# A vision tower's attention product in half-precision splits, tokens per column half, and steps moved in the tail

## The chip, the cores and the metric

The kernel runs on one core of a Trainium2 chip. The metric is the device time of one execution in microseconds, from the launch on the core to its end; the smaller the better. A core has TensorE (matrix products, accumulating in eight PSUM banks, here `bank[0]` to `bank[7]`), VectorE, ScalarE, GpSimd and the DMA queues of SyncE and GpSimd. Each engine works through its own list of instructions in order; they meet at semaphores, where one engine waits until another has counted up.

## The reference

Eight images of 3 x 256 x 256 in float32 go through three steps, with 256 tokens of 256 numbers per image:

```
gray  = weighted sum of the three colours
h     = (|scharr_x * gray| + |scharr_y * gray|) / 2      # 3x3 convolutions: tokens
Q,K,V = h Wq' + bq, h Wk' + bk, h Wv' + bv
h     = layernorm(h + softmax(causal(Q K' / 16)) V)
p     = softmax(h Wr);  e = argmax(p);  pos = rank of the token among those of e
kept  = pos < 320                                          # capacity of an expert
out   = where(kept, relu(h W1[e]) W2[e], h) * where(kept, max(p), 1)
h     = layernorm(h + out)
```

There are eight experts (256 to 1024 and back) with 320 slots each.

## The kernel before

**Halves.** A float32 matrix product takes TensorE several passes. Nearly all products are therefore made of two halves: `hi` is the number written in the type float32r, `lo` is the rest, number minus `hi`, and a product is hi hi + hi lo + lo hi, three matmuls of a faster kind. ScalarE writes a `hi` (ACTIVATE with Copy), and VectorE then the `lo` (a subtraction). The attention product, softmax weights times values, is the exception: `attend` (L1347) makes it of three full-precision matmuls, one for the first 128 tokens and two for the others, each with 264 columns (256 values and 8 gate columns, `XG`).

**The order of the work.** There are no planners: the source is five hand-written lists, one per engine, and the order of calls in a list is the order in time. In the attention stage, the loop `for i in range(B)` takes image i through attention, while image i+1 is convolved and i-1 is normalised and routed. On TensorE (L1380 on) it runs `project_keys(i)` (three terms of four matmuls; the third wants `xT_lo`), `project_values(i)`, `scores(i)` (three terms, the third wants the low keys, `yT_ready`), `count(i-1)`, the convolution of image i+1 for the two column halves of the picture (`convolve`, six groups of six matmuls; between the fifth and the sixth stand the transposes of the softmax weights, `prob_t`), `attend(i)` and `tokens_as_rows(i+1)`, four transposes of the tokens.

The steps of the other engines that the prediction names, with the names of the list and the tile as the profile shows it:

| step | engine, line | what it does |
|---|---|---|
| edges | ScalarE L609 | absolute value of one column half of the convolution, PSUM to `edges_abs` (in `tokens_mem`) |
| tokens | VectorE L907 | sum of both edge directions to `xT`, for both column halves at once |
| tokens_high, tokens_low | ScalarE L616, VectorE L912 | halves of `xT` (tiles `w_hi`, `w_lo`, which lend their space) |
| gray_high, gray_low | ScalarE L598, VectorE L860 | halves of the gray picture i+1 |
| project_keys, keys_low | ScalarE L623, VectorE L934 | halves of the keys with their bias, from bank 3 |
| project_values, row_constant | ScalarE L633, L639 | values out of PSUM to `val`; a constant per row |
| softmax_max | VectorE L959, L966 | scaled, masked scores and their maximum |
| probs, prob_t | ScalarE L649, L672 | exponentials; transposed weights out of bank 7 |
| route, residual, moments, assign, factor | VectorE L1009, L985, L992, L1036, L1029 | choice of expert, residual, layernorm statistics, slot of a token, gate factor |
| residual_in | VectorE L928 | token rows plus the value bias |
| route_exp, norm_rows, norm_lone | ScalarE L701, L680, L689 | exponentials of the gate; rows to scatter; rows for tokens without a slot |
| red_and_green, scale_blue, add_blue | VectorE L855, ScalarE L591, GpSimd L520 | gray picture i+2 |
| tally, scatter, scale_rows, scale_lone | GpSimd L498, L512, L465, L477 | running counts; two indirect DMAs that write an image's rows to their slots in DRAM; layernorm scales |
| split_high, split_low | ScalarE L712, VectorE L919 | halves of a quarter of an expert's weights, 128x1024 |

VectorE's list for image i is route(i-1), gray_low(i+1), factor(i-2), keys_low(i), residual(i-1), softmax_max(i), moments(i-1), residual_in(i), assign(i-1), softmax_sum(i), red_and_green(i+2), tokens(i+1), tokens_low(i+1). ScalarE's is gray_high(i+1), project_keys, project_values, row_constant, scale_blue(i+2), norm_lone(i-2), probs(i), edges(i+1, 0), prob_t(i), edges(i+1, 1), route_exp(i-1), tokens_high(i+1), norm_rows(i-1). The weights of expert 0 are split for the first time in images 5 and 6.

**The tail.** The last image, 7 (`L`), has a list of its own: `late_prob_t`, `late_attend`. Expert 0 gets its tokens partly from DRAM (`early_turn`, L1436, in which blocks of token rows are multiplied by the identity in full precision) and, for images 6 and 7, directly by `place` (L1423), a full-precision product of the rows with a 0/1 matrix `pick` that VectorE makes by comparisons in `assign`. Then the expert stage begins (L1208 to L1210), eight experts one after another.

## Time and profile before

| | us |
|---|---|
| median of three runs | 260.03 |
| lowest, highest | 259.54, 262.11 |
| the profiled execution | 262.5 |
| its span | 260.7 |
| busy: TensorE, VectorE, ScalarE, GpSimd | 243.5, 182.4, 155.3, 98.4 |

The profile is of one execution. A row of a timeline begins with the start in us from the beginning of the span and the duration; rows that follow one another closely are merged, with their number behind x. In brackets stands how long the engine was idle before it and which instruction ended the wait. Neighbouring instructions of an engine overlap by their fill and drain: the start of the next row, not the end of this one, gives the pace. The attention stage reaches from about 20 to 121 us, the expert stage to the end.

### The profile page before, as it was taken

The numbers are of one execution on the slowest core, as the hardware profiler recorded it, in microseconds if no ns is written. First come the engines' busy times: TensorE is split into PE (matmuls) and PEld (weight loads), VectorE is DVE, ScalarE is ACT, GpSimd is POOL, SyncE is SP. The second block draws the span as 40 slices with busy tenths as digits, with TensorE's granted clock in tenths as the row PEclk, the third lists the DMA queues.
The fourth block names the chain that finished last, engine by engine and source line by source line (L and its number), as shares of the span: only waits on it lengthen the run. The fifth ranks groups of instructions, "written<-read, shape, count | busy, mean of one in ns | idle before, by whom it ended". The sixth has DMA issues, their size and how long they took to land.

```text
span 260.7 us, 5010 instructions
## 1 busy us (share of the span) xinstructions
PE 243.5 (93%) x1690; PEld 227.9 (87%) x1690; DVE 182.4 (70%) x544; ACT 155.3 (60%) x351; POOL 98.4 (38%) x172
## 2 busy tenths in 40 slices
PE   6999999999999899898999999999999999999930
PEld 5999898989898798776999999999999999999930
DVE  4845496968778987965756696777967678777530
ACT  4325556776768687475645568474774748655400
POOL 6000116655665655646100025034250332513473
PEclk9989999999999999999999999999999999999995
DMA  6947192346595201041799807337092450100000
GB/s 191 268 120 252 28 299 52 115 137 226 179 373 186 73 20 60 29 131 41 199 261 334 298 5 263 112 97 259 0 296 78 150 203 3 46 0 23 10 27 0
DMA packets 28122, 35.48 MB, mean 136 GB/s; under 512 B 2652, under 2 KB 24907, under 8 KB 28098
## 3 DMA queue, kind: packets, MB, share of 16 engines
q1 hardware_dynamic: 26016, 31.71, 37.8%
q0 software_dynamic: 1792, 3.47, 3.7%
q8 instruction: 13, 0.21, 0.3%
q14 instruction: 11, 0.09, 0.1%
q10 hardware_dynamic: 290, 0.00, 0.1%
HBM read 26.97 MB, written 9.47 MB: 140 GB/s over the span
## 4 chain that ended last, share of the span: by engine, by line
PE 84%; DVE 6%; issue 3%; ACT 2%; POOL 2%; POOLq 1%; DMA 0%; ACTq 0%; DVEq 0%
PE bank L1208 16%; PE bank L1210 15%; PE bank L1209 15%; PE bank L1280 14%; PE bank L1296 5%; PE bank L1333 4%; PE bank L1455 3%; DVE xT L907 2%; PE bank L1506 2%; PE bank L1430 2%; PE bank L1370 2%; PE bank L1307 2%; ACT tokens_mem L609 1%; POOL out_dram L552 1%; PE bank L1216 1%
## 5 line engine op out<-in xcount | busy, mean ns | idle before, releaser
L1137 DVE SCALAR_TENSOR_TENSOR h_lo<-bank,h_hi 128x320 fp32r<-128x320 f32 x58 | 28.4, 490 | 29.3 <-ACT h_hi L782 25.5
L782 ACT ACTIVATE h_hi<-bank 128x320 fp32r<-128x320 f32 x58 | 25.4, 438 | 38.3 <-PE bank L1210 38.0
L1208 PE MATMUL bank<-einT_hi,w_hi 128*128 128x320 f32 x128 | 40.5, 317 | 0.3 <-DVE h_lo L1137 0.2
L1210 PE MATMUL bank<-einT_hi,w_lo 128*128 128x320 f32 x128 | 39.6, 309 | 0.0
L1209 PE MATMUL bank<-einT_lo,w_hi 128*128 128x320 f32 x128 | 39.5, 309 | 0.0
L919 DVE TENSOR_TENSOR w_lo<-w_raw,w_hi 128x1024 fp32r<-128x1024 f32 x32 | 38.9, 1216 | 0.0
L552 POOL DMA_INDIRECT out_dram<-tokens_mem,images x24 | 27.4, 1143 | 28.4 <-ACT tokens_mem L799 22.2
L1208 PE MATMUL bank<-h_hi,w_hi 128*128 128x320 f32 x112 | 35.4, 316 | 0.1
L1209 PE MATMUL bank<-h_lo,w_hi 128*128 128x320 f32 x112 | 34.6, 309 | 0.0
L1210 PE MATMUL bank<-h_hi,w_lo 128*128 128x320 f32 x112 | 34.6, 309 | 0.0
L712 ACT ACTIVATE w_hi<-w_raw 128x1024 fp32r<-128x1024 f32 x32 | 33.7, 1054 | 1.2 <-DMA w_raw<-in_L_ffn_W_dram 1.2
L546 POOL TENSOR_TENSOR yrstd<-yve,minus_half 128x3 f32<-128x3 f32 x7 | 6.2, 880 | 60.9 <-DVE yve L1167 60.7
L1208 PEld LDWEIGHTS bank<-einT_hi,w_hi 128*128 128x128 f32 x128 | 24.1, 188 | 1.0 <-DVE h_lo L1137 0.4
L1209 PEld LDWEIGHTS bank<-einT_lo,w_hi 128*128 128x128 f32 x128 | 24.1, 188 | 0.0
L1210 PEld LDWEIGHTS bank<-einT_hi,w_lo 128*128 128x128 f32 x128 | 24.0, 188 | 0.0
L1208 PEld LDWEIGHTS bank<-h_hi,w_hi 128*128 128x128 f32 x112 | 21.0, 188 | 0.8 <-issue 0.3
L1209 PEld LDWEIGHTS bank<-h_lo,w_hi 128*128 128x128 f32 x112 | 21.1, 188 | 0.0
L1210 PEld LDWEIGHTS bank<-h_hi,w_lo 128*128 128x128 f32 x112 | 21.0, 188 | 0.0
L512 POOL DMA_INDIRECT dispatched<-trow,slot x16 | 16.4, 1026 | 8.5 <-issue 7.8
L609 ACT ACTIVATE tokens_mem<-bank 128x512 f32<-128x512 f32 x16 | 9.6, 599 | 10.5 <-PE bank L1280 10.5
L1280 PE MATMUL bank<-w_hi 128*128 128x260 f32 x96 | 15.6, 300 | 0.0
L907 DVE TENSOR_TENSOR xT<-tokens_mem 128x512 f32<-128x512 f32 x8 | 6.7, 843 | 12.0 <-ACT tokens_mem L609 12.0
(228 smaller groups left out, 598.9 us busy)
## 6 DMA issues: line engine op xcount, KB each, us to landing
w_raw<-in_L_ffn_W_dram SPq DMA_DIRECT2D x16, 1024.0 KB
images<-in_x_dram SPq DMA_DIRECT2D x7, 768.0 KB, 5.0
dispatched<-blank SPq DMA_DIRECT2D x4, 645.0 KB, 8.7
images<-dispatched SPq DMA_DIRECT2D x9, 258.0 KB, 3.3
out_dram<-lone SPq DMA_DIRECT2D x8, 256.0 KB, 3.6
images<-in_x_dram SPq DMA_DIRECT2D x2, 384.0 KB, 4.9
images<-dispatched SPq DMA_DIRECT2D x9, 64.5 KB, 3.7
out_dram<-tokens_mem,images POOLq DMA_INDIRECT x24
```

Source lines behind the costliest of these rows:

```text
L512: pool.indirect_dma_start(dispatched, bass.IndirectOffsetOnAxis(ap=slot[:, b % TR, s:s + 1], axis=0), trow[:, b % TR, s, :], None, bounds_ ...
L552: pool.indirect_dma_start(out_rows, bass.IndirectOffsetOnAxis(ap=ein[0:n, e, j, D + 1:D + 2].bitcast(U32), axis=0), z[0:n, e % 2, j, :], N ...
L609: act.activation(edges_abs[:, c].rearrange("p f s -> p (f s)"), bank[c][:, :], ACT.Abs).then_inc(edges_ready, 1)
L712: act.activation(w_hi[:, e % 2, c], w_raw[:, e % 2, c], ACT.Copy).then_inc(w_hi_ready, 1)
L782: act.activation(hidden_halves(n)[0], bank[n % 2][:, 0:CAP], ACT.Relu).then_inc(h_hi_ready, 1)
L919: dve.tensor_tensor(w_lo[:, e % 2, c], w_raw[:, e % 2, c], w_hi[:, e % 2, c].bitcast(F32), ALU.subtract).then_inc(w_lo_ready, 1)
L1137: dve.scalar_tensor_tensor(lo, bank[n % 2][:, 0:CAP], 0.0, hi.bitcast(F32), ALU.max, ALU.subtract).then_inc(h_ready, 1)
L1208: pe.matmul(to, ah, bh, start=first, stop=False)
L1209: pe.matmul(to, ah, bl, start=False, stop=False)
L1210: return pe.matmul(to, al, bh, start=False, stop=last)
L1280: ins = pe.matmul(acc[:, :, s * (S - REACH):s * (S - REACH) + REACH], half[:, b % 2, s, c * P + dx:c * P + dx + P], of_band[:, dx, :, 2 - ...
L1296: ins = pe.matmul(bank[3][:, c * S:(c + 1) * S], half[:, k, c * P:(c + 1) * P], of_x[:, b % 2, k, :], start=(t == c == k == 0), stop=(t == ...
```

## The change

The attention product of images 0 to 5 is made by `attend_halves`: nine matmuls of the halves of the transposed weights and of the values. ScalarE writes the high halves (`values_high`, `prob_t_high`, the latter in place of `prob_t`), VectorE the low ones (`values_low`, `prob_t_low`). Images 6 and 7 keep the full-precision product. `edges`, `tokens`, `tokens_high`, the key projection's first term and `tokens_as_rows` now go by column half, with a semaphore count for each.

Steps are moved: on ScalarE gray_high behind project_keys, norm_lone behind probs, and the weight splits of image 5 to image 6; on VectorE the first token half ahead of assign, red_and_green behind the second token half, factor from the next image's list to behind red_and_green, and in the tail softmax_max ahead of moments, route ahead of factor, and `base` behind the comparisons; on GpSimd scatter ahead of tally; on TensorE early_turn ahead of place, now as real transposes, and two idle-filling matmuls (`keep_warm(2)`) are gone.

```diff
@@ -159,6 +161,8 @@
         probT = sb("probT", [P, S + P])
+        probT_hi = sb("probT_hi", [P, S + P], F32R)
+        probT_lo = sb("probT_lo", [P, S + P], F32R)
@@ -520,10 +528,10 @@
             for i in range(B):
+                if i >= 2:
+                    scatter(i - 2)
                 if i >= 1:
                     tally(i - 1)
-                if i >= 2:
-                    scatter(i - 2)
                 gate_tokens(i)
@@ -604,16 +612,28 @@
                 if b >= 1:
-                    act.wait_ge(xT_ready, b)
+                    act.wait_ge(xT_ready, DC * (b - 1) + c + 1)
                 act.wait_ge(conv_done, DC * b + c + 1)
...
-            def tokens_high(b):
-                act.wait_ge(xT_ready, b + 1)
+            def tokens_high(b, c):
+                act.wait_ge(xT_ready, DC * b + c + 1)
                 if b >= 2:
                     act.wait_ge(scores_done, b - 1)
-                act.activation(xT_hi[:, b % 2], xT[:, b % 2], ACT.Copy).then_inc(xT_hi_ready, 1)
+                act.activation(xT_hi[:, b % 2, c], xT[:, b % 2, c], ACT.Copy).then_inc(xT_hi_ready, 1)
+
+            def values_high(b):
+                if b >= 1:
+                    act.wait_ge(attn_done, b)
+                act.wait_ge(rowc_ready, b + 1)
+                act.activation(val_hi[:, :, :], val[:, b % 2, :, 0:XG], ACT.Copy).then_inc(val_hi_ready, 1)
+
+            def prob_t_high(b):
+                act.wait_ge(pT_done, b + 1)
+                if b >= 1:
+                    act.wait_ge(attn_done, b)
+                act.activation(probT_hi[:, :], bank[7][:, 0:S + P], ACT.Copy).then_inc(probT_hi_ready, 1)
@@ -730,31 +750,37 @@
             gray_high(1)
-            tokens_high(0)
+            for c in range(DC):
+                tokens_high(0, c)
             act.wait_ge(setup_ev, 1)
             for i in range(B):
+                project_keys(i)
                 if 1 <= i < L:
                     gray_high(i + 1)
-                project_keys(i)
                 project_values(i)
...
                 elif i < L:
-                    split_high(1)
+                    split_high(0)
                 if i == L:
                     break
+                if i < L - 1:
+                    values_high(i)
+                probs(i)
                 if i >= 2:
                     norm_lone(i - 2)
-                probs(i)
                 edges(i + 1, 0)
-                if i == L - 2:
-                    split_high(0)
-                prob_t(i)
+                tokens_high(i + 1, 0)
+                if i == L - 1:
+                    split_high(1)
+                    prob_t(i)
+                else:
+                    prob_t_high(i)
                 edges(i + 1, 1)
+                tokens_high(i + 1, 1)
                 if i >= 1:
                     route_exp(i - 1)
-                tokens_high(i + 1)
                 if i >= 1:
@@ -899,16 +925,26 @@
-            def tokens(b):
-
-                dve.wait_ge(edges_ready, DC * (b + 1))
+            def tokens(b, c):
+
+                dve.wait_ge(edges_ready, DC * b + c + 1)
                 if b >= 2:
                     dve.wait_ge(scores_done, b - 1)
-                dve.tensor_tensor(xT[:, b % 2], edges_abs[:, :, 0, :], edges_abs[:, :, 1, :], ALU.add
+                dve.tensor_tensor(xT[:, b % 2, c], edges_abs[:, c, 0, :], edges_abs[:, c, 1, :], ALU.add
                                   ).then_inc(xT_ready, 1)
+            def values_low(b):
+                dve.wait_ge(val_hi_ready, b + 1)
+                dve.tensor_tensor(val_lo[:, :, :], val[:, b % 2, :, 0:XG], val_hi[:, :, :].bitcast(F32), ALU.subtract
+                                  ).then_inc(val_lo_ready, 1)
+
+            def prob_t_low(b):
+                dve.wait_ge(probT_hi_ready, b + 1)
+                dve.tensor_tensor(probT_lo[:, :], bank[7][:, 0:S + P], probT_hi[:, :].bitcast(F32), ALU.subtract
+                                  ).then_inc(probT_lo_ready, 1)
+
             def tokens_low(b):
-                dve.wait_ge(xT_hi_ready, b + 1)
+                dve.wait_ge(xT_hi_ready, DC * (b + 1))
                 dve.tensor_tensor(xT_lo[:, b % 2], xT[:, b % 2], xT_hi[:, b % 2].bitcast(F32), ALU.subtract
@@ -1034,13 +1070,16 @@
                 step(dve.tensor_tensor(mine[:, :, :], onehot[:, b % 2], count, ALU.mult))
-                step(dve.tensor_scalar(base[:, :], best[:, b % 2], -float(CAP), float(E * CAP - 1),
-                                       ALU.mult, ALU.add))
+                if b < L - 1:
+                    step(dve.tensor_scalar(base[:, :], best[:, b % 2], -float(CAP), float(E * CAP - 1),
+                                           ALU.mult, ALU.add))
                 settle()
...
                                           ).then_inc(pick_ready, 1)
+                    step(dve.tensor_scalar(base[:, :], best[:, b % 2], -float(CAP), float(E * CAP - 1),
+                                           ALU.mult, ALU.add))
                 link(dve.tensor_reduce(place[:, :], mine[:, :, :], AX_X, ALU.add))
@@ -1069,7 +1108,8 @@
             make_gray(1)
-            tokens(0)
+            for c in range(DC):
+                tokens(0, c)
             gray_low(1)
@@ -1087,8 +1127,6 @@
                     gray_low(i + 1)
-                if i >= 2:
-                    factor(i - 2)
                 keys_low(i)
@@ -1097,29 +1135,36 @@
                 residual_in(i, 1)
+                tokens(i + 1, 0)
                 if i >= 1:
                 softmax_sum(i)
+                if i < L - 1:
+                    values_low(i)
+                    prob_t_low(i)
+                else:
+                    split_low(0)
+                tokens(i + 1, 1)
                 if i + 2 < B:
                     red_and_green(i + 2)
-                if i >= L - 2:
-                    split_low(i - L + 2)
-                tokens(i + 1)
+                if i >= 1:
+                    factor(i - 1)
+                if i == L - 1:
+                    split_low(1)
                 tokens_low(i + 1)
             route(L - 1)
-            factor(L - 2)
             residual(L - 1)
             keys_low(L)
+            softmax_max(L)
             moments(L - 1)
-            softmax_max(L)
             assign(L - 1)
             moments(L)
+            route(L)
             factor(L - 1)
-            route(L)
             assign(L)
@@ -1285,25 +1330,26 @@
             def project_keys(b):
-                pe.wait_ge(xT_hi_ready, b + 1)
                 if b >= 1:
...
                         pe.wait_ge(xT_lo_ready, b + 1)
-                    for c in range(DC):
-                        for k in range(DC):
+                    for k in range(DC):
+                        if t == 0:
+                            pe.wait_ge(xT_hi_ready, DC * b + k + 1)
+                        for c in range(DC):
                             ins = pe.matmul(bank[3][:, c * S:(c + 1) * S], half[:, k, c * P:(c + 1) * P],
...
             def tokens_as_rows(b):
-                pe.wait_ge(xT_ready, b + 1)
                 if b >= 1:
                     pe.wait_ge(xb_ready, b)
-                for s in range(SC):
-                    for c in range(DC):
+                for c in range(DC):
+                    pe.wait_ge(xT_ready, DC * b + c + 1)
+                    for s in range(SC):
                         ins = pe.transpose(bank[2][:, s * D + c * P:s * D + (c + 1) * P],
@@ -1344,8 +1390,23 @@
+            def attend_halves(b):
+                pe.wait_ge(probT_hi_ready, b + 1)
+                pe.wait_ge(val_hi_ready, b + 1)
+                for t, (p, v) in enumerate(((probT_hi, val_hi), (probT_hi, val_lo), (probT_lo, val_hi))):
+                    if t == 1:
+                        pe.wait_ge(val_lo_ready, b + 1)
+                    if t == 2:
+                        pe.wait_ge(probT_lo_ready, b + 1)
+                    for k in range(SC):
+                        pe.matmul(bank[5][:, 0:XG], p[:, (k + 1) * P:(k + 2) * P], v[:, k, :],
+                                  start=(t == k == 0), stop=(t == 2 and k == SC - 1))
+                for t, (p, v) in enumerate(((probT_hi, val_hi), (probT_hi, val_lo), (probT_lo, val_hi))):
+                    ins = pe.matmul(bank[7][:, 0:XG], p[:, 0:P], v[:, 0, :], start=(t == 0), stop=(t == 2))
+                ins.then_inc(attn_done, 1)
+
             def attend(b):
-                pe.wait_ge(probT_ready, b + 1)
+                pe.wait_ge(probT_ready, 1)
                 pe.matmul(bank[7][:, 0:XG], probT[:, 0:P], val[:, b % 2, 0, 0:XG], start=True, stop=True)
@@ -1394,7 +1455,10 @@
                     convolve(i + 1, 1, (2,))
-                    attend(i)
+                    if i < L - 1:
+                        attend_halves(i)
+                    else:
+                        attend(i)
                     tokens_as_rows(i + 1)
@@ -1408,7 +1472,7 @@
             def late_attend():
-                pe.wait_ge(probT_ready, L + 1)
+                pe.wait_ge(probT_ready, 2)
                 pe.matmul(bank[5][:, 0:XG], probT[:, P:2 * P], val[:, L % 2, 0, 0:XG], start=True, stop=False)
@@ -1421,31 +1485,29 @@
             def place(b):
-                if b == L - 1:
-                    pe.wait_ge(rowc_ready, B)
                 for c in range(DC):
...
                         ins = pe.matmul(bank[c][:, 0:CAP], trow[:, b % TR, s, c * P:(c + 1) * P], pick(b, s),
-                                        start=(b == L - 1 and s == 0), stop=(b == L and s == SC - 1),
+                                        start=False, stop=(b == L and s == SC - 1),
                                         skip_group_check=True)
...
             def early_turn():
+                pe.wait_ge(rowc_ready, B)
                 pe.wait_ge(ein_in[0], 32)
                         ins = pe.matmul(bank[c][:, o:o + n], ein[0:n, 0, j, c * P:(c + 1) * P], ident[0:n, 0:n],
-                                        start=False, stop=False, skip_group_check=True)
+                                        start=(j == 0), stop=False, is_transpose=True, skip_group_check=True)
                 ins.then_inc(early_turned, 1)
+            early_turn()
             place(L - 1)
-            early_turn()
             count(L)
             place(L)
-            keep_warm(2)
                 pe.wait_ge(ein_in[e], 32)
```

## Rows read from the trace of the kernel before

**Rows 1.** the trace's windows: each engine's busy us, then PEclk, DMA share, GB/s.

```profile
52.00:104.00 52.00, 50.70 (x387) 46.26 (x386) 41.29 (x160) 38.18 (x106) 31.50 (x57) 1.00 0.46 157
```

**Rows 2.** timeline of TensorE, image 4: start us, us, instruction, count, idle before.

```profile
68.61 0.64 PE L1296 MATMUL bank<-w_lo,w_hi 128*128 128x256 f32 x4
...
71.54 0.62 PE L1333 MATMUL bank<-w_hi,w_lo 128*128 128x128 f32 x4
...
76.94 0.71 PE L1349 MATMUL bank<-val,probT 128*128 128x264 f32 x2
...
78.65 0.66 PE L1307 MATMUL bank<-ident,xT 128*128 128x128 f32 x4
```

**Rows 3.** chain of waits in order of time: start us, us, what.

```profile
76.36 0.73 PE bank L1280 x6
```

**Rows 4.** timeline of VectorE, image 4.

```profile
69.48 0.69 DVE L860 TENSOR_TENSOR w_lo<-red,w_hi 128x512 fp32r<-128x512 f32 x1
...
70.17 0.88 DVE L934 SCALAR_TENSOR_TENSOR w_lo<-bank,key_bias,w_hi 128x256 fp32r<-128x256 f32 x2
...
72.19 0.29 DVE L959 CUSTOM_DVE_ANT_0 tokens_mem<-bank,causal 128x128 f32<-128x128 f32 x1 [0.37 <-PE bank L1333]
...
75.06 0.16 DVE L1036 TENSOR_TENSOR mine<-onehot,bank 128x16 f32<-128x16 bf16 x1
...
75.96 0.67 DVE L855 SCALAR_TENSOR_TENSOR red<-images 128x512 f32<-128x512 f32 x1
...
77.80 0.80 DVE L907 TENSOR_TENSOR xT<-tokens_mem 128x512 f32<-128x512 f32 x1 [1.16 <-ACT tokens_mem L609]
```

**Rows 5.** timeline of ScalarE, image 4.

```profile
68.39 0.61 ACT L598 ACTIVATE w_hi<-red 128x512 fp32r<-128x512 f32 x1
...
69.29 0.84 ACT L623 ACTIVATE w_hi<-bank,key_bias 128x256 fp32r<-128x256 f32 x2 [0.28 <-PE bank L1296]
...
72.20 0.93 ACT L689 ACTIVATE lone<-trow,lone_scale 128x256 f32<-128x256 f32 x2
...
74.67 0.60 ACT L609 ACTIVATE tokens_mem<-bank 128x512 f32<-128x512 f32 x1 [0.56 <-PE bank L1280]
...
77.17 0.60 ACT L609 ACTIVATE tokens_mem<-bank 128x512 f32<-128x512 f32 x1 [0.28 <-PE bank L1280]
...
78.14 0.19 ACT L701 ACTIVATION_READ_ACCUMULATOR lexp<-lsub,rstd 128x1 f32 x1
```

**Rows 6.** timeline, image 5, and instances of line L520: ns min/median/max, first and last start.

```profile
86.94 1.05 ACT L712 ACTIVATE w_hi<-w_raw 128x1024 fp32r<-128x1024 f32 x1
...
88.32 1.22 DVE L919 TENSOR_TENSOR w_lo<-w_raw,w_hi 128x1024 fp32r<-128x1024 f32 x1
...
L520 POOL TENSOR_TENSOR red<-red,images x6: 1266/1270/2112, 28.2 to 88.6; 128x512 f32<-128x512 f32 x6
...
89.60 1.61 DVE L907 TENSOR_TENSOR xT<-tokens_mem 128x512 f32<-128x512 f32 x1
...
91.27 0.66 PE L1307 MATMUL bank<-ident,xT 128*128 128x128 f32 x4 [0.93 <-DVE xT L907]
```

**Rows 7.** part 5 of the page: busy us, mean ns, idle us before it.

```profile
L512 POOL DMA_INDIRECT dispatched<-trow,slot x16 | 16.4, 1026 | 8.5 <-issue 7.8
```

**Rows 8.** timeline of TensorE, the first images.

```profile
20.24 0.63 PE L1307 MATMUL bank<-ident,xT 128*128 128x128 f32 x4 [0.27 <-DVE xT L907]
...
31.66 0.65 PE L1307 MATMUL bank<-ident,xT 128*128 128x128 f32 x4
```

**Rows 9.** timeline of the tail of the attention stage.

```profile
111.50 0.71 PE L1412 MATMUL bank<-val,probT 128*128 128x264 f32 x2 [0.19 <-ACT probT L664]
...
112.94 2.32 PE L1430 MATMUL bank<-tokens_mem,trow 128*128 128x320 f32 x8
...
115.09 1.97 PE L1440 MATMUL bank<-ident,images 128*128 128x128 f32 x12
...
117.32 0.17 DVE L1036 TENSOR_TENSOR mine<-onehot,bank 128x16 f32<-128x16 bf16 x1 [0.92 <-PE bank L1365]
```

More of the change, by code:

```diff
@@ L151, in vit_tower_kernel @@
         val = sb("val", [P, 2, SC, VCOLS - 2])
+        val_hi = sb("val_hi", [P, SC, XG], F32R)
+        val_lo = sb("val_lo", [P, SC, XG], F32R)
         gate_in = sb("gate_in", [P, 2, SC, E])
@@ L227, in vit_tower_kernel @@
         mean_done = sem("mean_done")
+        val_hi_ready = sem("val_hi_ready")
+        val_lo_ready = sem("val_lo_ready")
+        probT_hi_ready = sem("probT_hi_ready")
+        probT_lo_ready = sem("probT_lo_ready")
         late_probs_ready = sem("late_probs_ready")
```

## The prediction

> **What bounds the kernel now.** I read first the busy time and the granted clock of the stretch in which images 1 to 6 go through attention, then that stretch's timeline engine by engine, then the places where VectorE and GpSimd overlap, then the tail. TensorE is busy 50.70 of 52 us at full clock [rows 1]: the period of an image is the length of TensorE's work, and anything that makes TensorE wait is paid in full. The expert stage after it is one unbroken run of matmuls, so it passes a shift on and absorbs none. The attention stage decides.
>
> I use two marks for one image i (numbers of image 4 and the start of 5). Y is the end of its key projection: the third product starts at 68.61 and ends 0.64 later, 69.25 [rows 2]. S is the start of its softmax maximum on VectorE, 72.19, right behind the last score product [rows 2, 4]. From Y to S are 2.94 us. From S on, the next image's convolution ends when the attention product starts, 76.94 or S+4.75; the token transposes start at 78.65 and last 0.66, so they end at S+7.12 [rows 2]. Eight key matmuls later, at S+8.18, the low half of the tokens is needed, and Y of the next image is S+8.82.
>
> **The attention product.** Full-precision matmuls of 264 columns: three took 112.94 - 111.50 = 1.44 us in the late copy of this product [rows 9]. The half-precision convolution matmul has 260 columns and takes 0.73 / 6 = 0.122 us in the chain of waits [rows 3]; an upper end is 0.64 / 4 = 0.16, the last drain counted in, for the 256 columns of the key product [rows 2]. Nine are 1.10 to 1.44 us; I take 1.11, by the chain's row, whose columns are nearest. TensorE alone saves 0.33 us, and, as the transposes today also wait for xT (77.80 + 0.80 = 78.60, where 76.94 + 1.44 is 78.38) [rows 4], up to 0.25 more, since xT now comes in halves. Six images at 0.58: 3.5 us is the most that this part can give.
>
> **What the halves cost VectorE.** New work between S and the last token half: a 128x528 subtraction, between 0.67 us (512 elements, two tensor inputs, row of 75.96) and 1.22 (1024) [rows 4, 6], by size 0.71; a 128x384 subtraction from PSUM, between the 0.44 of one and the 0.88 of two subtractions of 256 from there (row of 70.17) [rows 4], by size 0.54; and the second start of the split xT, two pieces of about 0.4 (half of 0.67, and a start) against one of 0.80. The line of VectorE: from S to the end of the residual input it is 75.06 - 72.19 = 2.87. There it now waits for the first token half. ScalarE does the lone rows after the exponentials instead of before (0.93, the row of 72.20) [rows 5]. The exponentials end at 74.67 - 0.56 = S+1.92, so lone rows end at S+2.86 and the edges at S+3.46 instead of 75.27 = S+3.08. So tokens from S+3.48, then assign and sum (75.96 - 75.06 = 0.90), and the low values start at S+4.72 and are done at S+5.43; low probabilities, started 0.62 later, are done at S+5.90; the second token half at S+6.22. TensorE wants the low values at S+5.0 and the low probabilities 0.25 after those: it waits 0.45 and 0.2, ends attention at S+6.56 and the transposes at S+7.2. Against S+7.12: **+0.08 us an image**. The whole saving is eaten by the waits. Splitting the tokens' high copy costs ScalarE about 0.15 and lies in its idle time, for between the edges of 74.67 and of 77.17 it has only the probabilities' copy [rows 5], so I cost it at nothing; without that cover it would delay the high probabilities by as much.
>
> **The low tokens.** Red-and-green (0.67) is now between the second token half and the low tokens, and so is the factor, which waits for the routing exponentials. Those follow the second high copy on ScalarE: from S+6.57 to S+7.24 (0.66, from 77.77 less the overlap of 0.1 to 78.14 + 0.19) [rows 5]. The low tokens could start at S+7.38 and end at S+8.1, in time for S+8.26. But the blue plane's addition on GpSimd starts when red-and-green ends, about S+6.95, and its median is 1.27. Where it did meet two-tensor subtractions of VectorE, it took 2.11 from 88.6, while the subtraction of 88.32 kept its 1.22; then the xT of 89.60 took 1.61 in place of 0.80, and TensorE waited 0.93 [rows 6]. That is one waiting for the other, first GpSimd, then VectorE: behind the subtraction's end at 89.54 the addition still took 1.15. So here the low tokens really start at about S+8.1 and are done at S+8.75: **+0.6 us** an image for images 2 to 4, 0.5 in the first. Today the addition lies in VectorE's idle 1.16 us.
>
> The Trainium skill, "SBUF — State Buffer", section "SBUF: two separate sides", calls the ports that VectorE shares with GpSimd an exclusive lock, held for the whole instruction by whichever starts first, a VectorE operation with two SBUF inputs or a GpSimd one that reads SBUF. By that rule the low tokens wait as above; by free sharing they would not, and the sum would be the third case below. By that rule, the trace agrees.
>
> **The gray halves, in the other order.** ScalarE's gray_high moves behind project_keys; VectorE's gray_low stays before keys_low. Today gray_high runs at 68.39, before Y [rows 5], gray_low at 69.48, and keys_low at 70.17 [rows 4], as soon as the high keys (69.29 + 0.84) are there; it ends at 71.05, 0.49 before the third score product wants it at 71.54 [rows 2]. Now: high keys Y+0.79 in pitch, gray_high to Y+1.40, gray_low 0.6, keys_low from Y+2.02, done Y+2.90, where Y+2.29 is wanted. TensorE waits 0.61, scores end at Y+3.56, and the residual (0.79) puts S at Y+3.60 against 2.94. **+0.66 us for each of images 1 to 6: 3.96.** Nothing covers it: behind the scores, TensorE has only the count and the convolution queued.
>
> **Moved steps.** The two scattering transfers of an image, (16.4 + 8.5) / 8 = 3.1 us of GpSimd with their gaps [rows 7], now stand before the tally. With the addition later they run from about S+10 to S+13, the tally ends at S'+0.9 of the next image; its users (counts, one image later) and the next row scaling (S'+2.4) come after it: nothing. SP only waits on those landings at the end. Image 5 no longer carries a weight split, so what its wait of 0.93 is above the others' goes [rows 6]: **-0.85**, less the 0.6 above. Image 6 carries both: on ScalarE the second split (1.05) [rows 6] stands before the probabilities' copy, which ends about S+5.7 instead of S+4.7, so the full-precision attention starts 1 us late; on VectorE a split of 1.22 stands before the low tokens, done at S+9.55, wanted at S+8.9. Y comes at S+10.2 against about S+8.75: **+1.5**. Image 0 has neither lone rows nor factor: transposes end at about 31.84 against 31.66 + 0.66 [rows 8]: **-0.48**. Before it, the 0.27 us wait for xT [rows 8] goes: **-0.25**.
>
> **The tail.** Today early_turn takes 1.91 us behind place (115.09 to 117.0) and the count of image 7 stands behind it, while VectorE, done with the one-hot at 117.32 - 0.92 = 116.40, waits for the count [rows 9]. As six transposes (0.66 / 4 each) in front of place it takes 1.0: 0.5 off. Base behind the comparisons gives 0.2. Maximum before moments would give 0.4 on the critical side, but keys_low comes 0.3 later, and moments then stands before the last residual: +0.3. **-0.6** in sum. The two warming matmuls had filled a wait: nothing.
>
> **Sum.** -0.25 - 0.48 + 3.96 + 0.5 + 3 x 0.6 + (0.6 - 0.85) + 1.5 - 0.6 = +6.2 us. It is made on the profiled execution (262.5 us, span 260.7, so 1.8 around it), which is 2.5 us above the median of the runs, 260.03; the difference is put on the median: **266.2 us**.
>
> **Rivals.** (a) *Everything covered, faster.* If gray_low and the low halves landed before TensorE wants them, 0.58 would be won per image: the sum with -0.58 in place of the terms of images 1 to 5, no 3.96, gives -3.6, 256.4. It decides at keys_low done by Y+2.29: it would need 0.6 us less between Y and keys_low, and both orders and durations speak against it. For it: VectorE has 1.16 us idle per image in one piece [rows 4]. 0.08. (b) *Only gray binds*: the low values and probabilities arrive by S+5.25, say because the edges are not delayed and subtractions run nearer their lower bounds, and the low tokens slip in before the addition. Then -2.3 - 1.4 for images 1 to 5 against 3.96 and 1.5 and the ends: +0.4, 260.4. 0.12. (c) *No lock between VectorE and GpSimd*: the low tokens are on time, images 1 to 4 cost about nothing and image 5 gives 0.75: +3.5, 263.5. Against it stands the overlap [rows 6], for it only that it is one event. 0.15. (d) *TensorE's clock falls in the new waits*, about 1.3 us an image in three or four pieces. The clock has two levels, 1.2 and 2.4 GHz; the stretch shows only the upper. Against it: 0.93 of idle at 90.3 left the clock at 1.00 [rows 1, 6]. One convolution part of 0.73 at half speed per image is 4.4 on top: 270.6. 0.08. The forecast keeps 0.57, by itself 264.5 to 268.5: the ends are the 528-element subtraction up to 0.98 (+0.27 x 5) and matmuls of 0.16 (+0.3 x 5) above, and a lock that costs only half below.
>
> **Numbers.** About 1% (2.6 us) is what a measurement can tell from none. Faster by it: 0.08, case (a). Within: 0.14, case (b) and a corner of (c). Slower: 0.78, the rest. The range, 260 to 269, leaves out (a), (d) and some of (b).
>
> **What the profile after would show.** TensorE waiting before the third score product for keys_low (w_lo), about 0.6 us, six times; before the second and third attention products; before the third key product for the low tokens, those lasting about 1.3 in place of 0.7 beside the blue addition; image 7's key projection ending some 7 us later than 105.3; the count no longer behind early_turn. The prediction is wrong if the third score product starts without a wait, or if the period from image to image stays at or under 11.8 us.

## The result and the profile after

The changed kernel takes 268.18 us (median of four runs, 267.75 to 268.64); the kernel before, on the same chip, 259.95. The ratio is 1.027, with a 95% interval of 1.022 to 1.033: 8.2 us slower, where 6.2 were forecast. The profiled execution took 267.75 us with a span of 266.0. Executions of every kernel here fall on two levels, 2.3 us apart (262.0 and 259.7 us for the kernel before), of which the profiles show the upper one with 0.50 and the lower one with 1.00 of TensorE's clock granted from 13 to 15 us, ahead of the attention stage; the profile before lies on the upper level and all four executions of the changed kernel on the lower, so "at equal starts" below means medians of the lower level. The spans of the two profiles therefore differ by 5.3 us only, and I compare them by marks inside the attention stage.

The window of the attention stage, in the columns of [rows 1]:

```profile
52.00:104.00 52.00, 46.87 (x369) 43.60 (x369) 43.84 (x162) 36.19 (x103) 27.47 (x55) 1.00 0.47 157
```

TensorE is busy 46.87 of 52 us in place of 50.70, at the same clock; VectorE 43.84 in place of 41.29. The work shrank and the waits grew. The timeline of TensorE shows them for the same image as [rows 2]:

```profile
68.86 0.74 PE L1342 MATMUL bank<-w_lo,w_hi 128*128 128x256 f32 x4 [0.77 <-DVE w_lo L948]
...
72.56 0.73 PE L1379 MATMUL bank<-w_hi,w_lo 128*128 128x128 f32 x4 [0.52 <-DVE w_lo L970]
...
78.08 0.51 PE L1402 MATMUL bank<-val_hi,probT_hi 128*128 128x264 f32 x2
...
78.54 0.51 PE L1402 MATMUL bank<-val_lo,probT_hi 128*128 128x264 f32 x2
...
79.01 0.51 PE L1402 MATMUL bank<-val_hi,probT_lo 128*128 128x264 f32 x2
...
79.72 0.60 PE L1353 MATMUL bank<-ident,xT 128*128 128x128 f32 x4
...
80.07 0.72 PE L1342 MATMUL bank<-w_hi 128*128 128x256 f32 x4
```

The third key product waits 0.77 us for the low tokens, the third score product 0.52 us for the low keys (w_lo of line 970). In [rows 2] the key and score products had no wait. From one set of transposes to the next (66.53 to 79.72) it is 13.19 us; before, the marks Y of images 4 and 5 lay 11.76 us apart.

Within the attention product the second and third groups start 0.46 and 0.47 us after the one before. What they need without a wait is seen in image 0, where both lows come in time:

```profile
26.75 0.51 PE L1402 MATMUL bank<-val_hi,probT_hi 128*128 128x264 f32 x2
27.10 0.41 PE L1402 MATMUL bank<-val_lo,probT_hi 128*128 128x264 f32 x2
27.35 0.51 PE L1402 MATMUL bank<-val_hi,probT_lo 128*128 128x264 f32 x2
...
28.06 0.60 PE L1353 MATMUL bank<-ident,xT 128*128 128x128 f32 x4
```

There the steps are 0.35 and 0.25, and the whole product takes 1.31 us (26.75 to 28.06). In image 4 it takes 1.64 (78.08 to 79.72): 0.11 of waiting for the low values and 0.22 for the low weights. VectorE and then GpSimd in image 4, as in [rows 4] and [rows 6]:

```profile
67.28 0.17 DVE L1065 RECIPROCAL trow<-lsum 128x2 f32<-128x2 f32 x1 [0.45 <-ACT lexp L721]
...
67.36 1.44 DVE L948 TENSOR_TENSOR w_lo<-xT,w_hi 128x512 fp32r<-128x512 f32 x1
...
71.02 0.69 DVE L886 TENSOR_TENSOR w_lo<-red,w_hi 128x512 fp32r<-128x512 f32 x1 [0.89 <-ACT w_hi L606]
...
71.63 0.87 DVE L970 SCALAR_TENSOR_TENSOR w_lo<-bank,key_bias,w_hi 128x256 fp32r<-128x256 f32 x2
...
77.80 0.69 DVE L938 TENSOR_TENSOR val_lo<-val,val_hi 128x528 fp32r<-128x528 f32 x1
...
78.40 0.55 DVE L943 TENSOR_TENSOR probT_lo<-bank,probT_hi 128x384 fp32r<-128x384 f32 x1
```

```profile
66.97 1.28 POOL L528 TENSOR_TENSOR red<-red,images 128x512 f32<-128x512 f32 x1 [3.12 <-DVE red L881]
```

The low tokens (line 948) take 1.44 us in place of 0.7 because the blue addition has been running since 66.97. gray_low (line 886) comes behind 0.89 us of idleness, keys_low only behind it. The low values (0.69) and low weights (0.55) stand one behind the other at 77.80; the first are done at 78.49, and TensorE wanted them at 78.43.

The last loss is in no part of the attention stage. A timeline of all engines where it ends:

```profile
122.21 1.21 POOL L520 DMA_INDIRECT dispatched<-trow,slot  x1 [1.45 <-ACT trow L700]
...
127.33 1.24 DVE L955 TENSOR_TENSOR w_lo<-w_raw,w_hi 128x1024 fp32r<-128x1024 f32 x1
...
127.56 1.06 POOL L486 TENSOR_TENSOR v2n<-v,mv 128x2 f32<-128x2 f32 x1
...
128.98 1.70 POOL L490 TENSOR_TENSOR lone_scale<-v2e,minus_half 128x2 f32<-128x2 f32 x1
...
130.71 0.91 ACT L709 ACTIVATE lone<-trow,lone_scale 128x256 f32<-128x256 f32 x2 [2.56 <-POOL lone_scale L490]
...
132.52 0.42 PE L1253 MATMUL bank<-einT_hi,w_hi 128*128 128x320 f32 x1 [0.93 <-DVE h_lo L1182]
```

GpSimd's scatter of image 6 starts at 122.21. Its small scale operations therefore come at 127.56 and 128.98, beside weight splits on VectorE (one is the row of 127.33), and take 1.06 and 1.70 us. In the kernel before, the same two took 0.20 and 1.75 there, so only the first meeting is new; the first scale operation also comes 0.8 us later, counted from the first expert product. ScalarE writes the last lone rows behind them, the hidden block of expert 0 stands behind those, and TensorE waits 0.93 us.

### The profile page after: what moved, and what is told of

Its sections match the earlier page's. It is cut to its first block, busy times and chain, and to the rows that moved or that the text cites. A ratio compares the mean times of both kernels' runs of the same rounds, so it can differ in the third digit from the quotient of the medians.

```text
span 266.0 us, 5088 instructions
## 1 busy us (share of the span) xinstructions
PE 240.7 (90%) x1700; PEld 225.7 (85%) x1700; DVE 193.3 (73%) x564; ACT 159.3 (60%) x365; POOL 95.9 (36%) x172
## 4 chain that ended last, share of the span: by engine, by line
PE 44%; DVE 6%; POOL 5%; issue 4%; ACT 2%; POOLq 1%; DVEq 0%; ACTq 0%
PE bank L1253 14%; PE bank L1255 13%; PE bank L1254 13%; PE bank L1517 3%; PE bank L1568 2%; POOL out_dram L560 1%; POOL dispatched L520 1%; DVE resid L1021 1%; POOL yrstd L583 1%; POOL lone_scale L490 1%; POOLq L67 1%; PE bank L1379 1%; DVE stats L1028 1%; DVE w_lo L955 0%; DVE w_lo L970 0%
## 5 line engine op out<-in xcount | busy, mean ns | idle before, releaser
L520 POOL DMA_INDIRECT dispatched<-trow,slot x16 | 16.5, 1034 | 9.3 <-ACT trow L700 5.6
L528 POOL TENSOR_TENSOR red<-red,images 128x512 f32<-128x512 f32 x6 | 8.1, 1345 | 23.3 <-DVE red L881 23.3
L1325 PE MATMUL bank<-w_hi 128*128 128x260 f32 x96 | 14.9, 291 | 0.0
L1325 PE MATMUL bank<-w_lo,w_hi 128*128 128x260 f32 x96 | 14.9, 291 | 0.0
```

Source lines behind the costliest of these rows:

```text
L520: pool.indirect_dma_start(dispatched, bass.IndirectOffsetOnAxis(ap=slot[:, b % TR, s:s + 1], axis=0), trow[:, b % TR, s, :], None, bounds_ ...
L528: pool.tensor_tensor(red[:, b % 2], red[:, b % 2], pix[:, b % 2, 2], ALU.add).then_inc(gray_ready, 1)
L1325: ins = pe.matmul(acc[:, :, s * (S - REACH):s * (S - REACH) + REACH], half[:, b % 2, s, c * P + dx:c * P + dx + P], of_band[:, dx, :, 2 - ...
```

## The experiments

Diffs are against the changed kernel unless said otherwise. Ratios are to the kernel before, run in between on the same chip. The changed kernel itself was not run again beside them; at equal starts the kernel before reads 259.9, 259.8, 259.7 and 259.7 us in the four sessions, so a difference of two or three tenths from its 268.2 means nothing.

**e1_gray_first: one order undone.**

```diff
-                project_keys(i)
                 if 1 <= i < L:
                     gray_high(i + 1)
+                project_keys(i)
```

> The changed kernel (268.2 us) with gray_high again ahead of project_keys on ScalarE, nothing else. Theory (each of the six low-key waits of TensorE, 0.52 us, and the 0.2 us by which the residual then delays the softmax, is caused by this order): the wait before the third score product goes, the period falls from 13.18 to about 12.4 us, the time to about 263.5 us (-4.7). Rival 1 (VectorE is simply too loaded; the wait moves to the next place): the period stays above 12.9 and the time above 266.5. Rival 2 (the low tokens behind the blue addition set the period alone): no change.

264.5 us, ratio 1.014 (1.006 to 1.022): 3.7 us less. No third score product of images 1 to 6 waits any more, and the marks of the third key product lie 12.4 us apart. The low tokens keep their wait:

```profile
67.93 0.74 PE L1342 MATMUL bank<-w_lo,w_hi 128*128 128x256 f32 x4 [0.79 <-DVE w_lo L948]
```

The theory holds: images 2 to 6 gain 0.79 us each, as expected. Image 1 gains only 0.25, since it has a new wait of 0.31 for the high keys, and 4.2 us are won between the first and the last token transposes. The rest of the gap to the 4.7 expected is no effect of the edit: those first transposes start at 17.77 in this profile and at 16.87 in that of the changed kernel, though the steps ahead of them are the same.

**e2_low_first: low tokens ahead of what had been put in front of them.**

```diff
                 tokens(i + 1, 1)
+                tokens_low(i + 1)
                 if i + 2 < B:
                     red_and_green(i + 2)
                 if i >= 1:
                     factor(i - 1)
                 if i == L - 1:
                     split_low(1)
-                tokens_low(i + 1)
```

> The changed kernel with tokens_low directly behind the second token half on VectorE, ahead of red_and_green, factor and the second weight split. Theory (the low tokens are late because they stand behind red_and_green and then wait for the blue addition on GpSimd): the waits before the third key product (0.87, 0.72, 0.77, 0.77, 0.77 and, for image 7, 0.90 us) go, low tokens take 0.7 us instead of 1.45, time about 263.6 us (-4.6). Rival (the wait for high keys and gray halves behind it absorbs an earlier start): under 1.5 us gained.

263.85 us, ratio 1.010 (1.006 to 1.014): 4.3 less. All six waits before the third key product are gone, those before the third score product stay and are longer, 0.61 to 0.98 us in images 1 to 6:

```profile
70.67 0.73 PE L1379 MATMUL bank<-w_hi,w_lo 128*128 128x128 f32 x4 [0.65 <-DVE w_lo L970]
```

**e4_factor_first: the tail's factor put back.**

```diff
-            route(L)
             factor(L - 1)
+            route(L)
             assign(L)
```

> The changed kernel with factor(L-1) again ahead of route(L) in the tail of VectorE. Theory: GpSimd's scatter of image 6 waits for this factor; it started at 122.2 instead of about 119.9, so the scale of the last lone rows met two weight splits on VectorE (1.06 and 1.70 us) and ScalarE, with norm_lone in front of the second hidden block, held TensorE for 0.93 us. Then the scatter starts some 1.2 us earlier or more, that wait goes, and the time falls by about 1.2 us to 267.0. Rival (the wait comes from image 7's rows, which end GpSimd's queue anyhow, or from weight splits): no change.

267.0 us, ratio 1.022 (1.015 to 1.029): 1.2 less, and the wait of 0.93 is gone. The timeline shows how:

```profile
121.69 1.08 POOL L520 DMA_INDIRECT dispatched<-trow,slot  x1 [0.70 <-ACT trow L700]
...
127.09 0.19 POOL L486 TENSOR_TENSOR v2n<-v,mv 128x2 f32<-128x2 f32 x1
...
127.65 1.69 POOL L490 TENSOR_TENSOR lone_scale<-v2e,minus_half 128x2 f32<-128x2 f32 x1
...
129.37 0.91 ACT L709 ACTIVATE lone<-trow,lone_scale 128x256 f32<-128x256 f32 x2 [1.00 <-POOL lone_scale L490]
```

The scatter starts only 0.5 us earlier than at 122.21, less than I had expected. That is enough for the first small operation to slip in ahead of the split (0.19 us, not 1.06); the lone rows come 1.34 us earlier. One meeting is avoided, the other (1.69) stays, as in the kernel before.

**e5_blue_waits: the contention by itself.** One more wait, no operation moved within its engine.

```diff
                 pool.wait_ge(warm_ready, b - 1)
+                pool.wait_ge(xT_lo_ready, b)
```

> The changed kernel with one more wait: GpSimd's blue addition starts only when the low tokens of the image are done. No operation is removed or reordered within an engine. Theory (the low tokens, 1.45 us, wait inside their own time for the addition, which holds ports that both need): they take about 0.7 us, TensorE's wait before the third key product falls from 0.77 to about 0.1, the time by 0.65 us for each of images 2 to 6, to about 265 us. Rival (the low tokens are slow for another reason, or wait for the factor only): duration and time unchanged, or later because the gray picture comes later.

265.0 us, ratio 1.016 (1.009 to 1.024): 3.1 us less by adding a wait. The low tokens and the addition in this kernel:

```profile
66.22 0.67 DVE L949 TENSOR_TENSOR w_lo<-xT,w_hi 128x512 fp32r<-128x512 f32 x1
...
67.06 1.29 POOL L529 TENSOR_TENSOR red<-red,images 128x512 f32<-128x512 f32 x1 [4.35 <-DVE w_lo L949]
```

0.67 us in place of 1.44, and TensorE waits before no third key product but that of image 7. The theory holds. The transposes lie 12.4 us apart in place of 13.18, 0.78 an image where 0.65 was expected; the first ones start 0.4 us later than in the profile of the changed kernel.

**g4_before_gray: the gray order alone, on the kernel before.**

```diff
+                project_keys(i)
                 if 1 <= i < L:
                     gray_high(i + 1)
-                project_keys(i)
```

> The kernel before with one move alone: gray_high(i+1) behind project_keys(i) on ScalarE. Theory (the order by itself makes the low keys 0.6 us late and the residual behind them delays the softmax): 0.66 to 0.75 us for each of images 1 to 6, together +4.0 to +4.5 us, ratio about 1.016; TensorE waits 0.5 us before the third score product six times. Rival (in the kernel before the wait for xT would shrink by as much, or the chip needs the heavier VectorE line of the changed kernel to show it): under 1.5 us.

266.1 us, ratio 1.018 (1.011 to 1.025). Six waits of 0.52 to 0.58 before the third score product, as forecast. At equal starts (264.8, two executions, against 259.7) it is 5.1 us, a little more than forecast.

**g2_halves_only: the half-precision product alone, on the kernel before**, with norm_lone behind the first edges.

```diff
                 softmax_sum(i)
+                if i < L - 1:
+                    values_low(i)
+                    prob_t_low(i)
                 if i + 2 < B:
                     red_and_green(i + 2)
...
-                    attend(i)
+                    if i < L - 1:
+                        attend_halves(i)
+                    else:
+                        attend(i)
```

> The kernel before with the half-precision attention product of images 0 to 5 alone (and norm_lone behind the first edges, to make room for values_high); tokens whole, no step moved but that. VectorE makes the low values and weights behind softmax_sum, ahead of red_and_green and tokens. Theory (TensorE saves 0.33 us an image, but then waits for xT, which is now as late as before or later because 1.1 us of subtractions stand ahead of it): within 1 us of the kernel before. Rival (the saving arrives in full): 0.33 x 6 = 2 us faster.

264.2 us, ratio 1.014 (1.009 to 1.019): 4.4 us slower at equal starts, which neither theory had. Rows of TensorE, of VectorE, again of TensorE, and the window behind it (the columns of [rows 1]):

```profile
76.53 0.66 PE L1345 MATMUL bank<-ident,xT 128*128 128x128 f32 x4 [0.33 <-DVE xT L932]
...
89.34 1.75 DVE L932 TENSOR_TENSOR xT<-tokens_mem 128x512 f32<-128x512 f32 x1
...
91.15 1.12 PE L1345 MATMUL bank<-ident,xT 128*128 128x128 f32 x4 [2.52 <-DVE xT L932]
```

```profile
91.00:94.00 3.00, 2.85 (x14) 2.86 (x15) 2.17 (x11) 2.13 (x4) 1.93 (x5) 0.50 0.00 0
```

The product is shorter, but the transposes wait 0.33 us for xT in each of images 0 to 4, as the theory says: 0.17 an image slower than e6_tail_only, whose attention stage is that of the kernel before, 0.85 in all. What it missed is image 5, which carries a weight split on VectorE: the blue addition takes 2.11 us between that split and xT, xT takes 1.75, and TensorE waits 2.52 us in place of 0.93. From transposes to transposes image 5 takes 2.0 us more. Behind that wait TensorE is granted 0.50, the lower of its two levels, from 91 to 94 us: from the start of the transposes to the first value product it is 3.36 us (91.15 to 94.51), where the kernel before needs 2.20 at 1.00. The clock takes another 1.2 us. The three add up to 4.0, the difference of the two spans. How much of image 5's loss is the split rather than the halves was not separated; the kernel before had that split and the wait of 0.93 too, and kept its clock.

**e7_full: the changed kernel with the full-precision product.**

```diff
-                    if i < L - 1:
-                        attend_halves(i)
-                    else:
-                        attend(i)
+                    attend(i)
```

(and no values_high, values_low, prob_t_high, prob_t_low)

> The changed kernel with the full-precision attention product for all images again (no attend_halves, no high and low halves of values and weights), every moved step and the column halves of the tokens kept. Theory: TensorE pays 0.33 us more per image, but VectorE is 1.2 us lighter and ScalarE 0.6, so the low tokens come earlier by about 0.2 to 0.5; about 267.3 us, 0.5 to 1.5 less than the changed kernel: the halves gave nothing here. Rival (the halves are a gain that the moved steps hide): 2 us more, 270.

269.3 us, ratio 1.031 (1.027 to 1.035), 269.1 at equal starts against 268.2: 0.9 more, where I had expected less. The sign is a miss. In images 2 to 6 the period is the same 13.18 us, with 0.95 in place of 0.77 of waiting for the low tokens. From the first transposes to image 2's third key product it is 0.4 us longer, and the wait of 0.93 in the expert stage is 1.20.

**f1_best and f2_best_lone: three orders mended, then a fourth.**

```diff
-                if 1 <= i < L:
-                    gray_low(i + 1)
                 keys_low(i)
                 if i >= 1:
                     residual(i - 1)
+                if 1 <= i < L:
+                    gray_low(i + 1)
...
-                if i >= 2:
-                    norm_lone(i - 2)
                 edges(i + 1, 0)
+                if i >= 2:
+                    norm_lone(i - 2)
```

(with the moves of e2 and e4; the second hunk only in f2_best_lone. The gray order is mended on the other side here: gray_high stays, and VectorE's gray_low goes behind the low keys.)

> The changed kernel with three orders mended together: gray_low on VectorE behind keys_low and residual (gray_high stays behind project_keys), tokens_low directly behind the second token half, factor(L-1) ahead of route(L). Theory (the three effects are separate and add: -3.7, -4.3, -1.2 as measured one by one): about 259 us, at or 1 us under the kernel before. Rival (the same slack is counted twice): above 262.

> The kernel f1_best with norm_lone on ScalarE behind the first edges instead of ahead of them, so that the first token half comes 0.4 us earlier on VectorE and the low values and low weights with it. Theory (TensorE waits inside the attention product because VectorE's line from the softmax maximum is too long, and the edges were 0.4 of it): 0.4 us less per image of 2 to 5, about 257.4 us. Rival (the inner waits cost nothing since the token halves set the end): same as f1_best.

f1_best: 260.3 us, ratio 0.995 (0.992 to 0.997). f2_best_lone: 258.6, ratio 0.992 (0.988 to 0.995). At equal starts it is 260.2 and 258.5 against 259.7. The three effects, 3.7, 4.3 and 1.2, would give 259.0 if they added; they fall 1.3 us short. The period is 11.9 us in f1_best, still above the 11.76 before: the attention product waits for the low values 0.33 us in each of images 2 to 5. With the edges moved it is 11.54, which is the 0.4 an image that was expected: 1.7 us.

**f3_full_same_order: what the halves are worth, once the orders are right.** f2_best_lone with the full-precision product.

> The kernel f2_best_lone (258.6 us) with the full-precision attention product for all images, every order kept. Theory: with the three orders mended the period is TensorE's work again, so the product's own 0.33 us an image is what the halves give: 1.5 to 2 us more than f2_best_lone, 260.3. Rival (VectorE's 1.2 us of subtractions still hold TensorE as much as they save): the same as f2_best_lone or faster.

258.9 us, ratio 0.993 (0.990 to 0.997), not to be told from f2_best_lone; the rival had it. The attention product and the transposes behind it in f2_best_lone, then here, with the third score product of the same image:

```profile
73.56 0.50 PE L1402 MATMUL bank<-val_hi,probT_hi 128*128 128x264 f32 x2
...
74.14 0.51 PE L1402 MATMUL bank<-val_lo,probT_hi 128*128 128x264 f32 x2
...
75.32 0.60 PE L1353 MATMUL bank<-ident,xT 128*128 128x128 f32 x4
```

```profile
68.37 0.73 PE L1372 MATMUL bank<-w_hi,w_lo 128*128 128x128 f32 x4
...
73.90 0.71 PE L1403 MATMUL bank<-val,probT 128*128 128x264 f32 x2
...
75.34 0.60 PE L1346 MATMUL bank<-ident,xT 128*128 128x128 f32 x4
```

From 73.56 to 75.32 are 1.76 us, from 73.90 to 75.34 are 1.44. The halves' product is the longer one: 1.31 of matmuls and 0.45 of waiting for both lows. The full-precision kernel loses as much elsewhere: its third score product starts 0.71 us behind the second (67.66) and not 0.46, because the low keys come later. So both have a period of 11.54 us against 11.76 before, and what f2_best_lone gains over the kernel before is gained without the halves.

**e6_tail_only: the new tail on the kernel before**, without the move of factor (softmax_max and base are moved as well).

```diff
-            place(L - 1)
             early_turn()
+            place(L - 1)
             count(L)
             place(L)
-            keep_warm(2)
```

> The kernel before with the changed tail alone: early_turn ahead of place and as transposes, softmax_max of image 7 ahead of moments, base behind the comparisons, keep_warm(2) gone; factor stays where it was, the attention stage is untouched. Theory (0.5 us of early_turn, 0.4 of the maximum, 0.2 of base): 1.0 us less than the kernel before, ratio about 0.996. Rival (the late product and the count wait for VectorE anyway, as moments now stands before the last residual): within 0.3 us of the kernel before.

260.2 us, ratio 1.000 (0.996 to 1.004): no gain, as its rival had it but for another reason. The rows of GpSimd and TensorE:

```profile
103.90 1.07 POOL L512 DMA_INDIRECT dispatched<-trow,slot  x1 [0.67 <-issue]
...
110.95 1.18 PE L1442 MATMUL bank<-ident,images 128*128 128x128 f32 x6 [1.13 <-DMA images<-dispatched]
```

The rows of expert 0 are not back from DRAM when the tail wants them: 1.13 us. The scatter of image 5, which is the last that they need, stands behind the tally here and starts 3.87 us behind image 7's token transposes (100.03); in the changed kernel it stands ahead of the tally and starts 2.30 us behind them, and this wait is absent. So the scatter ahead of the tally, which the prediction costed at nothing, seems to be what lets the tail save its half microsecond; no run moved it alone.

**g1_late: the second weight split out of the way**, with the moves of f2_best_lone.

```diff
-                    split_high(1)
...
                     route_exp(i - 1)
+                if i == L - 1:
+                    split_high(1)
...
-                if i == L - 1:
-                    split_low(1)
...
             factor(L)
+            split_low(1)
```

> The kernel f2_best_lone with the second weight split out of the way: split_high(1) on ScalarE behind the routing exponentials of image 6 instead of ahead of the weights' copy, split_low(1) on VectorE behind the last factor instead of ahead of image 7's routing. Theory: TensorE's wait of 0.71 us before the full-precision product of image 6 and the 1.04 us before image 7's third score product go: about 1.7 us less than f2_best_lone, 256.9 us, the fastest of all. Rival (VectorE is late again at the start of the expert stage, where the split must be done): same as f2_best_lone.

258.3 us, ratio 0.991 (0.987 to 0.994), the lowest median, but only 0.3 us under f2_best_lone where 1.7 were expected, too little to tell the two apart. Both waits went, and the same wait as in e6_tail_only took their place:

```profile
99.36 1.04 ACT L732 ACTIVATE w_hi<-w_raw 128x1024 fp32r<-128x1024 f32 x1
...
102.23 1.07 POOL L520 DMA_INDIRECT dispatched<-trow,slot  x1 [3.58 <-ACT trow L700]
...
109.27 1.18 PE L1503 MATMUL bank<-ident,images 128*128 128x128 f32 x6 [1.14 <-DMA images<-dispatched]
```

The edit brought it about itself: the split of 99.36 now stands on ScalarE ahead of norm_rows, whose rows the scatter of image 5 waits for. The scatter starts 3.73 us behind image 7's transposes (98.50), in f2_best_lone 2.30.

## Why the prediction was right, point by point

From the rows of the two profiles, the increments between marks:

| step | forecast us | measured us |
|---|---|---|
| before the end of image 0's keys | -0.25 | -0.6 |
| image 0 | -0.48 | -0.47 |
| first image with both waits (Y of 1 to Y of 2) | +1.16 | +1.49 |
| the three images after it | +3.78 | +4.21 |
| Y of 5 to Y of 6 | +0.41 | +0.58 |
| Y of 6 to Y of 7 | +2.16 | +2.18 |
| tail to the first expert product | -0.6 | -0.5 |
| start of the expert stage | 0 | +1.3 |
| sum | +6.2 | +8.2 |

(The first row is against e6_tail_only, which has the steps of the kernel before there and an equal start. It is the weakest: among e1, e2, e4 and e5, whose steps there are those of the changed kernel, the first transposes start between 17.14 and 17.77, so 16.87 is an early one.)

**Gray order.** Right in place and cause: the wait stands where it was put, six times, and e1 and g4 show that this order alone makes it. The low keys are done at Y+2.90 (71.63 + 0.87), exactly as forecast. The idle time of 0.52 us is not comparable with the forecast's 0.61; counted from the pace of the kernel before, 0.46 behind the second product, the third starts 0.68 us late. From Y to S it is 3.72 us (69.60 to 73.32) against 3.60 forecast. The term was mis-sized by 0.12 us an image, because the group starts 0.06 us behind the low keys and is itself longer behind a wait (0.73 against 0.62 us); e1 gives 3.7 back, g4 adds 5.1.

**Low tokens.** Right: done at S+8.67 where S+8.75 was forecast, and e5 shows that the contention is the cause. Y of the next image is S+9.46 against 9.42.

**Attention product.** Forecast: its whole saving eaten by waits. That came true, with both parts mis-sized. The nine matmuls take 1.31 us without a wait, not 1.11, so TensorE saves 0.13 us an image and not 0.33; the waits are 0.11 and 0.22, not 0.45 and 0.2. In sum 1.64 us against 1.76. The low values and weights took 0.69 and 0.55 us where 0.71 and 0.54 were estimated; the second is luck, since by the two durations that the prediction names (0.44 and 0.88) 384 elements would be 0.66. The transposes end at S+6.75, 0.45 earlier than forecast, because they themselves take 0.35 us and not 0.66, which nothing in the prediction had; that only lengthened the next wait. f3 confirms that the product gives no time even in a good order.

**Splits.** Right: image 6 ends its next key projection at S+10.12 against S+10.2, though the full-precision product is 0.73 us late and not 1. **Image 0.** Right to 0.02 us by luck: of the 0.47 won, 0.31 is the shorter transposes, 0.13 the product (forecast 0.33) and 0.19 the earlier xT (0.15), and about 0.2 is lost again ahead of the product. **Tail.** The half microsecond came; VectorE waits 0.29 us for image 7's count in place of 0.92. It came on a condition that the prediction had not seen (e6).

**What failed.** The prediction gives route ahead of factor in the tail no term at all. It did not ask who waits for factor: the scatter of image 6 on GpSimd, whose queue ends with the last lone scale, which ScalarE needs ahead of a hidden block. That was 1.3 us by the marks, and e4 gives 1.2 of it back. With the 0.9 us by which the image terms were small it makes up the 2 us between forecast and result.

**The rivals.** Faster, and only-gray, fell with the first profile; that there is no lock fell with e5. The clock of the attention stage stayed at 1.00 through all waits of the changed kernel, the longest 0.90 us. That rival is no empty one, though: behind the 2.52 us of g2_halves_only the clock fell and cost 1.2 us.

## What to carry to other kernels

Before shortening the bounding engine's work by giving the next one more, follow the helper's line from the event that starts it to the piece that is wanted, in a period: here 0.13 us saved on TensorE met 1.2 us put on VectorE's line. And take the price of the new work from a place where it runs unhindered: nine matmuls at the pace of a longer run would be 1.1 us and are 1.31. When an order on one engine is changed, look at the other engine's list for the partner step that stayed, as gray_low did. And for every moved step, ask which queue waits for its result and what stands last in that queue.

## What the hardware showed unexpectedly

An added wait made a kernel 3.1 us faster (e5), by keeping a GpSimd addition out of the way of a VectorE subtraction. The same blocking hits tiny operations: in f2_best_lone a comparison of 128x16 with two inputs took 0.91 us in place of 0.17, beside the addition:

```profile
65.68 0.91 DVE L1050 TENSOR_TENSOR hit<-gate,lmax 128x16 f32<-128x16 f32 x1
```

```profile
65.26 1.30 POOL L528 TENSOR_TENSOR red<-red,images 128x512 f32<-128x512 f32 x1 [4.14 <-DVE red L881]
```

The Trainium skill, "SBUF — State Buffer", section "SBUF: two separate sides", says the port pair is locked for a whole instruction; by that rule the length of the blocked operation does not matter, and the trace agrees.

Four token transposes took 0.35 us from the first to the next product (79.72 to 80.07) when ordered by column half, and 0.66 in the kernel before, at the same clock. g2_halves_only with whole tokens has 0.66, f3_full_same_order with column halves 0.35, so it comes with the column halves and not with the product; whether the order of the four or the wait between them makes it was not separated.

The nine matmuls of the halves take 1.31 us in image 0 and not nine times the 0.12 of the convolution's: the second group of two starts 0.35 us behind the first, the product's last three matmuls start 0.35 behind the third group and then follow at 0.12. g2_halves_only, with whole tokens, shows the same steps. No run says what the two longer steps are.
